# Loads and statistics of the next image's first strips moved to an earlier stage, column means moved beside the sampling, group products cut from nine blocks to seven

## The chip, the cores and the metric

The kernel runs on one core of a Trainium2 chip. The metric is the device time of one execution in microseconds (us); smaller is better. TensorE (PE) has a granted clock of 1.2 or 2.4 GHz; the profile gives it as a share of full speed.

## The reference

The input `x` is (4, 384, 56, 56), float32. Two residual layers follow each other. Cut to what matters:

```python
def _gn(v, G=32, eps=1e-5):            # group norm: 32 groups of 12 channels, over the image
    g = v.reshape(B_, G, C_ // G, H_, W_)
    m = mean(g, axis=(2, 3, 4)); s = var(g, axis=(2, 3, 4))
    return ((g - m) / sqrt(s + eps)).reshape(v.shape)

x = x + layer0(_gn(x))   # depthwise 3x3 convs give value, query (56x56), key, offsets (28x28);
                         # value is sampled bilinearly at tanh(offsets), then attention without
                         # softmax (query x key, x sampled value) and a 384x384 output weight
x = x + layer1(_gn(x))   # layernorm + fc1 (384->1536), silu, fc2; qkv, normalised q and k,
                         # k^T v state per head, normalised output, projection
```

Layer 0 thus needs the mean and variance of every 12-channel group of the raw input before its convolutions; layer 1 needs the same of layer 0's output. fc1's weight is scaled by the layernorm's gain and has its column means taken off, once per launch.

## The kernel before

Channels lie on partitions in three chunks of 128 (`KC = 3`). An image is cut into seven strips of 8 rows, `T = 448` pixels (`STRIPS = 7`). Every engine's program is written out by hand, and the engines meet at semaphores; the order of the calls in each engine's block is the order of its work.

**Stages.** Image 0's layer 0 is a stage of its own (the lead-in, in the text below also "the front"). In it TensorE does nineteen strips of depthwise convolution with diagonal weights (`front_taps`, L826) while VectorE does the rest of the convolutions as units of eight taps each (`unit_conv`, L2086; units 0 to 3 are values, 4 to 6 queries; units 0 to 5 are half images, unit 6 two strips). Each value unit is transposed by TensorE, copied by ScalarE in four pieces into `VP` (L1486), and stored by SyncE's queue into `pair_scr` (`store_front_values`, L409). ScalarE's fourth piece reuses the first piece's buffer, so it waits for the first piece's store to land; only then does it start the unit two further on (`front_unit_start`, L1477). When the last store has landed, GpSimd issues fourteen indirect loads of sample points (`gather`, L666), two for each of seven tiles. VectorE mixes each tile (`sample_tile`, L1989 and L1992), TensorE multiplies it with the keys (`key_value`, L898); after the seventh come `key_value_heads` (MT, L1998), `key_value_out` (L942), and `W2TL`.

**The strip loop of layer 0.** Then seven strips follow (`project_strip` on TensorE). For strip t: SyncE loads queries `CQ` (L430) and the residual `CX` (L433); ScalarE rounds `CH` (`project_high`, L1559); VectorE makes `CL` (`project_low`, L2011); TensorE does 27 matmuls of 448 columns (L780 to L782); VectorE adds into `CX` (`project_add`, L2018) and takes statistics of the sum (L2021); SyncE stores `CX` into `x_scr` (L471). In SyncE's program `CQ` of strip t+2 is loaded in the turn of strip t, behind the store of strip t-1, which waits for that strip's additions. TensorE's strip t+1 uses the banks of strip t, and so waits for its additions. In the same loop VectorE also does `centre_columns` (L2094) in three strips, TensorE `column_means` (L808) after the first three strips, and both are followed by ScalarE's `W1H` (L1596).

**The statistics of the next image's input.** ScalarE's queue loads seven strips of `x` of image 1 into three rotating buffers `X0S` (`load_x0`, L329), and VectorE takes their statistics (`strip_stats`, L1901) inside the strip loop. For later images the same is done elsewhere with `X0Q`.

**The group norm's coefficients.** `gn_coefs` on VectorE and `gn_groups` on TensorE (L766, L774) work in turn: two sets of nine small matmul blocks (3 output chunks x 3 input chunks, a 128x128 block of the group matrix each, 4 columns) and short VectorE steps between them. This happens five times in a launch: at its start, behind the strip loop of image 0, and at the end of the second layer of images 0, 1 and 2 (the tails), among fc1 and fc2 matmuls. After it, `kv_start` normalises the first tile of layer 1 and TensorE starts its key and value products (L985 to L987).

Of the kernel before, what the change touches and what calls it, by code (L numbers as in the profile page):

```python
# [12 lines left out]
P = 128  # L13
C, H, W = 384, 56, 56
KC = C // P
# [58 lines left out]
def build(nc, d, out):  # L74
# [22 lines left out]
    with ctx:  # L97
# [159 lines left out]
        at = [base2]  # L257
        X0S = sb("X0S", [P, 3, KC, T], at=at)
        assert at[0] <= stats_at
# [64 lines left out]

        def load_x0(eng, g, t):

            if t >= 3:
                eng.wait_ge(s["x0bn"], g * STRIPS + t - 2)
            eng.dma_start(X0S[:, t % 3, :, :].rearrange("p k (r w) -> p k r w", w=W),  # L329
                          xin_v[g, :, :, 1 + t * RS:1 + (t + 1) * RS, :]).then_inc(s[f"x0_ld{t % 3}"], 16)  # L330
# [39 lines left out]
        def _(sp):  # L370
# [108 lines left out]
            for u in range(2, 4):  # L479
                store_front_values(u)  # L480
            for u in (4, 5):
                sp.wait_ge(s[("q_st", "q_st1")[u % 2]], (FQ - STRIPS) // 2 * 16)
                store_front_queries(u)
# [5 lines left out]
            load_queries(0)  # L489
            load_queries(1)  # L490
# [255 lines left out]
        def _(pe):  # L746
# [13 lines left out]
            def gn_groups(g, pa, pb, between=None):  # L760

                pe.wait_ge(s["grp_ld"], g * 16 + 16)
                pe.wait_ge(s["gn_st"], g + 1)
                for ko in range(KC):
                    for ki in range(KC):
                        last = mm(pa[:, 4 * ko:4 * ko + 4], grp[:, ki, ko * P:(ko + 1) * P],  # L766
                                  gst[:, ki, :, :].rearrange("p s c -> p (s c)"), start=(ki == 0), stop=(ki == KC - 1))
                last.then_inc(s["gn_mm"], 1)
                if between is not None:
                    between()  # L770
                pe.wait_ge(s["gn_dev"], g + 1)
                for ko in range(KC):
                    for ki in range(KC):
                        last = mm(pb[:, 4 * ko:4 * ko + 4], grp[:, ki, ko * P:(ko + 1) * P],  # L774
                                  gdev[:, ki, :, :].rearrange("p s c -> p (s c)"), start=(ki == 0), stop=(ki == KC - 1))
                last.then_inc(s["gn_mm2"], 1)
# [182 lines left out]
            for t in range(len(SUM_AT), STRIPS):  # L959
                key_value(0, t, VSP)  # L960
            key_value_out(0)
            for t in range(STRIPS):
                project_strip(0, t)
                if t < KC:
                    column_means(t)
# [405 lines left out]
        def _(act):  # L1371
# [217 lines left out]
            load_x0(act, 1, 0)  # L1589
            load_x0(act, 1, 1)  # L1590
            for t in range(2, STRIPS):
                load_x0(act, 1, t)
                project_high(0, t)
                if t == STRIPS - 2:
                    act.wait_ge(s["set_ctr"], 1)
                    fn(W1H[:, :, :], fc1w[:, :, :], ACT.Copy).then_inc(s["w_h"], 1)  # L1596
# [288 lines left out]
        def _(dve):  # L1885
# [10 lines left out]
            def strip_stats(g, t, x=None):  # L1896

                x = X0S[:, t % 3, :, :] if x is None else x
# [232 lines left out]
            unit_conv(4, 3, 6)  # L2131
            for t in range(4):
                sample_tile(0, t, GP, VSP)
            unit_conv(5, 1, 8)
            unit_conv(6, 1, 8)
# [12 lines left out]
            for t in range(STRIPS):  # L2148
                if t == STRIPS - 1:
                    strip_stats(1, t)  # L2150
                project_add(0, t)
                if t + 2 < STRIPS:
                    project_low(0, t + 2)
                if 1 <= t <= KC:
                    centre_columns(t - 1)
                if t < STRIPS - 1:
                    strip_stats(1, t)
# [433 lines left out]
```

## Time and profile before

| what | value |
|---|---|
| median of 3 runs | 2768.92 us (2767.82 to 2769.37) |
| profiled execution, its own time | 2791.05 us |
| its span | 2789.2 us |
| PE busy | 2687.2 us, 96% |
| DVE (VectorE) busy | 1978.9 us, 71% |
| ACT (ScalarE) busy | 1169.6 us, 42% |
| mean granted TensorE clock | 0.969 |

The profiled execution is 22.1 us longer than the median of the runs, so differences are worked out inside it and then laid to the median. The page's 40 slices show TensorE full nearly everywhere except in the first 320 us, where DMA traffic is at its highest.

### The profile page before, as it was taken

The page shows a single profiled execution, that of the slowest core. Times are in us where ns is not written, and L with a number is a line of the kernel's source. Part 1 is how long each engine was busy: PE and PEld are TensorE (multiplying, and loading weights), DVE is VectorE, ACT ScalarE, POOL GpSimd, SP SyncE. Part 2 cuts the span into 40 slices and gives each one's busy share as a digit, 9 for nine tenths or more (in the row PEclk, how much of TensorE's full clock was granted, in tenths as well). Part 3 has the DMA queues.
Part 4 walks back from the last instruction along what each step waited for, and adds up shares of the span by engine and source line. Part 5 has one row for each costly group of instructions (what it writes and reads, how often), then busy time and mean ns, then how long its engine had stood idle before and what let it go on. Part 6 is the DMA issues. An engine that isn't in the chain of part 4 may idle for free.

```text
span 2789.2 us, 36724 instructions
## 1 busy us (share of the span) xinstructions
PE 2687.2 (96%) x14382; PEld 2444.5 (88%) x14382; DVE 1978.9 (71%) x2513; ACT 1169.6 (42%) x2035; POOL 655.7 (24%) x219
## 2 busy tenths in 40 slices
PE   6998799999999999999999999999999999999999
PEld 4556799999998899999998899999998899999998
DVE  4988785988887685988887685988887534434343
ACT  3432465444442465444442366444442253333332
POOL 0020142222232043222223042322224033211210
PEclk8998899999999999999999999999999999999999
DMA  5257643343338642334337743333346632112110
GB/s 224 59 151 246 207 129 83 105 114 114 102 108 258 215 132 75 103 106 115 123 91 231 241 140 84 102 102 102 104 124 204 232 101 70 44 44 57 44 43 30
DMA packets 208249, 345.52 MB, mean 124 GB/s; under 512 B 24272, under 2 KB 191824, under 8 KB 205392
## 3 DMA queue, kind: packets, MB, share of 16 engines
q1 hardware_dynamic: 182048, 309.87, 34.3%
q10 hardware_dynamic: 21552, 14.05, 3.7%
q0 software_dynamic: 4480, 19.27, 2.4%
q8 instruction: 115, 1.88, 0.3%
q14 instruction: 54, 0.44, 0.1%
HBM read 239.59 MB, written 103.56 MB: 123 GB/s over the span
## 4 chain that ended last, share of the span: by engine, by line
PE 74%; DMA 7%; issue 7%; DVE 5%; POOL 4%; ACT 2%; SPq 0%; ACTq 0%; DVEq 0%; POOLq 0%
PE bank L780 16%; PE bank L781 16%; PE bank L782 16%; PE bank L826 3%; PE bank L985 3%; PE bank L987 3%; PE bank L986 3%; PE bank L1008 3%; PE bank L1176 3%; DMA r_scr<-rr 3%; POOL rq L702 2%; PE bank L1162 2%; DVE AC L2391 1%; PE bank L1120 1%; POOL ro L706 1%
## 5 line engine op out<-in xcount | busy, mean ns | idle before, releaser
L1750 ACT ACTIVATE S<-bank,b1p 128x448 f32<-128x448 f32 x336 | 212.4, 632 | 819.5 <-PE bank L782 752.5
L2391 DVE SCALAR_TENSOR_TENSOR AC<-XV,wfold,AC 128x1568 f32<-128x1568 f32 x288 | 530.0, 1846 | 11.5 <-ACT AC L1782 8.9
L780 PE MATMUL bank<-SH,W2H 128*128 128x448 f32 x1008 | 389.9, 387 | 0.2
L780 PE MATMUL bank<-XRH,W1H 128*128 128x448 f32 x1008 | 376.8, 374 | 1.3 <-ACT S L1750 1.3
L781 PE MATMUL bank<-SL,W2H 128*128 128x448 f32 x1008 | 374.0, 371 | 0.0
L782 PE MATMUL bank<-SH,W2L 128*128 128x448 f32 x1008 | 373.7, 371 | 0.0
L781 PE MATMUL bank<-XRL,W1H 128*128 128x448 f32 x1008 | 373.2, 370 | 0.0
L782 PE MATMUL bank<-XRH,W1L 128*128 128x448 f32 x1008 | 371.9, 369 | 0.0
L702 POOL TENSOR_TENSOR rq<-qn,nhalf 112x32 f32<-112x32 f32 x28 | 181.9, 6498 | 481.0 <-DVE qn L2330 481.0
L2360 DVE TENSOR_TENSOR SL<-S,SH 128x448 fp32r<-128x448 f32 x336 | 207.1, 618 | 87.7 <-ACT SH L1753 87.7
L706 POOL TENSOR_TENSOR ro<-on,nhalf 112x32 f32<-112x32 f32 x28 | 180.2, 6434 | 298.7 <-DVE on L2351 298.6
L694 POOL TENSOR_TENSOR rk<-kn,nhalf 128x16 f32<-128x16 f32 (+1 forms) x64 | 169.8, 2667 | 272.0 <-DVE kn L2173 272.0
L985 PE MATMUL bank<-WKVH,XH 128*128 128x384 f32 (+1 forms) x600 | 209.5, 349 | 14.9 <-DVE XL L2030 13.5
L780 PEld LDWEIGHTS bank<-XRH,W1H 128*128 128x128 f32 x1008 | 193.5, 192 | 18.5 <-ACT S L1750 2.1
L1753 ACT ACTIVATE SH<-S 128x448 fp32r<-128x448 f32 x336 | 194.4, 578 | 31.7 <-ACT S L1750 1.1
L782 PEld LDWEIGHTS bank<-XRH,W1L 128*128 128x128 f32 x1008 | 192.1, 191 | 17.4
L782 PEld LDWEIGHTS bank<-SH,W2L 128*128 128x128 f32 x1008 | 194.6, 193 | 14.4
L780 PEld LDWEIGHTS bank<-SH,W2H 128*128 128x128 f32 x1008 | 193.8, 192 | 14.6 <-DVE SL L2360 1.3
L781 PEld LDWEIGHTS bank<-XRL,W1H 128*128 128x128 f32 x1008 | 192.7, 191 | 15.2
L781 PEld LDWEIGHTS bank<-SL,W2H 128*128 128x128 f32 x1008 | 194.7, 193 | 12.2 <-issue 0.6
L986 PE MATMUL bank<-WKVL,XH 128*128 128x384 f32 (+1 forms) x600 | 203.9, 340 | 0.0
L987 PE MATMUL bank<-WKVH,XL 128*128 128x384 f32 (+1 forms) x600 | 203.9, 340 | 0.0
(227 smaller groups left out, 5169.0 us busy)
## 6 DMA issues: line engine op xcount, KB each, us to landing
XV<-in_xp SPq DMA_DIRECT2D x36, 870.0 KB, 6.9
XC<-in_xp SPq DMA_DIRECT2D x13, 1682.0 KB, 9.2
CQ<-q_scr SPq DMA_DIRECT2D x28, 672.0 KB
CX<-in_x SPq DMA_DIRECT2D x28, 672.0 KB, 5.2
x_scr<-CX SPq DMA_DIRECT2D x28, 672.0 KB, 5.7
X<-x_scr SPq DMA_DIRECT2D x28, 672.0 KB, 4.2
V<-v_scr SPq DMA_DIRECT2D x28, 672.0 KB, 7.3
Y<-x_scr SPq DMA_DIRECT2D x28, 672.0 KB
```

What stands on the lines that cost most here:

```text
L702: pool.tensor_tensor(rq[:, :], qn[:, :], nhalf[0:TS, :], ALU.pow).then_inc(s["rq_s"], 1)
L706: pool.tensor_tensor(ro[:, :], on[:, :], nhalf[0:TS, :], ALU.pow).then_inc(s["ro_s"], 1)
L780: mm(o, wh, xh, start=first, stop=False)
L781: mm(o, wh, xl, start=False, stop=False)
L782: return mm(o, wl, xh, start=False, stop=stop)
L985: mm(p, xh, WKVH[:, k, c0:c0 + C], start=(k == 0), stop=False)
L986: mm(p, xh, WKVL[:, k, c0:c0 + C], start=False, stop=False)
L987: last = mm(p, xl, WKVH[:, k, c0:c0 + C], start=False, stop=(k == KC - 1))
L1750: fn(S[:, j % 2, :], bank[j % 2][:, 0:T], ACT.Silu, bias=b1p[:, j:j + 1]).then_inc(s["s_s"], 1)
L1753: fn(SH[:, j % 3, :], S[:, j % 2, :], ACT.Copy).then_inc(s["sh"], 1)
L2360: tt(SL[:, j % 3, :], S[:, j % 2, :], f(SH[:, j % 3, :]), ALU.subtract).then_inc(s["sl"], 1)
L2391: stt(o, XV[h][:, ky:ky + HR, kx:kx + W], wfold[:, kind, k, 3 * ky + kx:3 * ky + kx + 1], o, ALU.mult, ALU.add).then_inc(s["va"], 1)
```

## The change

1. `X0S` and `load_x0` go. The seven strips of image 1 are loaded by SyncE's queue into the single buffer `CQ1`, which the queries use only later; each load but the first waits for the statistics of the strip before it. The loads stand ahead of or between the stores of value units 2 and 3, and the last five ahead of the stores of query units 4 and 5.
2. VectorE's seven `strip_stats(1, t, CQ1)` move from the strip loop to between the convolution units 4, 5 and 6; the first two taps of unit 5 move ahead of the first four sample tiles.
3. `column_means` 0 to 2 move from behind the first three strips to ahead of the last three `key_value`; `centre_columns` goes one strip earlier, ahead of the additions.
4. `load_queries(1)` waits for the last strip's statistics too.
5. In every `gn_groups`, each output chunk multiplies only neighbouring input chunks: seven blocks in place of nine. The two left out (0 with 2) are zero in the group matrix, as a group has 12 neighbouring channels.

```diff
-        def load_x0(eng, g, t):
-            if t >= 3:
-                eng.wait_ge(s["x0bn"], g * STRIPS + t - 2)
-            eng.dma_start(X0S[:, t % 3, :, :]..., xin_v[g, :, :, 1 + t * RS:1 + (t + 1) * RS, :])...
...
+            def load_first_strip(t):
+                if t >= 1:
+                    sp.wait_ge(s["x0bn"], STRIPS + t)
+                sp.dma_start(CQ1[:, :, :].rearrange("p k (r w) -> p k r w", w=W),
+                             xin_v[1, :, :, 1 + t * RS:1 + (t + 1) * RS, :]).then_inc(s[f"x0_ld{t % 3}"], 16)
+            sp.wait_ge(s["wkv_st"], 32)
+            load_first_strip(0)
+            store_front_values(2)
+            load_first_strip(1)
+            store_front_values(3)
+            for t in range(2, STRIPS):
+                load_first_strip(t)
+            sp.wait_ge(s["q_st"], (FQ - STRIPS) // 2 * 16)
+            store_front_queries(4)
+            sp.wait_ge(s["q_st1"], (FQ - STRIPS) // 2 * 16)
+            store_front_queries(5)
...
             load_queries(0)
+            sp.wait_ge(s["x0bn"], 2 * STRIPS)
             load_queries(1)
...
+                near = ((0, 1), (0, 1, 2), (1, 2))
                 for ko in range(KC):
-                    for ki in range(KC):
+                    for ki in near[ko]:
...
             for t in range(len(SUM_AT), STRIPS):
+                column_means(t - len(SUM_AT))
                 key_value(0, t, VSP)
             for t in range(STRIPS):
                 project_strip(0, t)
-                if t < KC:
-                    column_means(t)
...
             sampling_points(0)
-            unit_conv(4, 3, 6)
+            strip_stats(1, 0, CQ1)
+            unit_conv(4, 3, 3)
+            strip_stats(1, 1, CQ1)
+            unit_conv(4, 6, 3)
+            strip_stats(1, 2, CQ1)
+            unit_conv(5, 1, 2)
             for t in range(4):
                 sample_tile(0, t, GP, VSP)
-            unit_conv(5, 1, 8)
-            unit_conv(6, 1, 8)
+            strip_stats(1, 3, CQ1)
+            unit_conv(5, 3, 3)
+            strip_stats(1, 4, CQ1)
+            unit_conv(5, 6, 3)
+            strip_stats(1, 5, CQ1)
+            unit_conv(6, 1, 4)
+            strip_stats(1, 6, CQ1)
+            unit_conv(6, 5, 4)
...
             for t in range(STRIPS):
-                if t == STRIPS - 1:
-                    strip_stats(1, t)
+                if t < KC:
+                    centre_columns(t)
                 project_add(0, t)
                 if t + 2 < STRIPS:
                     project_low(0, t + 2)
-                if 1 <= t <= KC:
-                    centre_columns(t - 1)
-                if t < STRIPS - 1:
-                    strip_stats(1, t)
```

## Rows read from the trace of the kernel before

**Rows 1.** Stages: us, busy us per engine (x instructions), PE clock, DMA share, GB/s.

```profile
160.00:165.00 5.00, 5.00 (x17) 2.65 (x16) 4.89 (x4) 4.29 (x5) 0.00 (x0) 1.00 1.00 271
...
200.00:205.00 5.00, 5.00 (x21) 2.94 (x21) 3.15 (x6) 0.00 (x0) 3.78 (x5) 1.00 1.02 291
...
242.00:304.00 62.00, 53.65 (x213) 42.67 (x213) 52.89 (x85) 12.62 (x10) 0.00 (x0) 0.92 0.94 320
280.00:285.00 5.00, 5.00 (x14) 4.44 (x14) 4.06 (x7) 1.32 (x1) 0.00 (x0) 0.50 0.96 264
...
321.00:960.00 639.00, 629.77 (x3493) 590.67 (x3494) 508.02 (x627) 290.25 (x510) 169.50 (x53) 0.98 0.45 135
```

**Rows 2.** VectorE's strip loop: start, us, operation, [idle before, releaser].

```profile
275.61 1.88 DVE L2094 TENSOR_TENSOR fc1w<-fc1w,bank 128x512 f32<-128x512 f32 x3
277.41 1.67 DVE L1901 BATCH_NORM_STATS2 bst<-X0S 128x6 f32<-128x448 f32 x3
279.00 1.66 DVE L2018 TENSOR_TENSOR CX<-CX,bank 128x448 f32<-128x448 f32 x3
...
283.19 1.56 DVE L2011 TENSOR_TENSOR CL<-CQ,CH 128x1344 fp32r<-128x1344 f32 x1 [0.94 <-ACT CH L1559]
...
304.82 1.36 DVE L1908 BATCH_NORM_AGGREGATE gst<-bst 128x2 f32<-128x42 f32 x6
```

**Rows 3.** Transfer sizes from 140 to 320 us, and SyncE's and ScalarE's timeline.

```profile
X0S<-in_x ACTq DMA_DIRECT2D x7, 672.0 KB, 10.2
...
160.25 23.74 SPq L409 DMA_DIRECT2D pair_scr<-VP  x8
...
264.20 0.51 SPq L430 DMA_DIRECT2D CQ<-q_scr  x1
...
272.78 1.33 ACT L1559 ACTIVATE CH<-CQ 128x1344 fp32r<-128x1344 f32 x1 [7.62 <-DMA CQ<-q_scr]
```

**Rows 4.** ScalarE in the front: the pieces of the value units, and the scaling of fc1's weight.

```profile
167.90 0.60 ACT L1486 ACTIVATE VP<-bank 112x512 f32<-112x512 f32 x1 [3.60 <-DMA pair_scr<-VP]
168.40 1.96 ACT L1477 ACTIVATE AP<-XC,bfold,wfold 128x784 f32<-128x784 f32 x2
...
228.38 4.51 ACT L1584 ACTIVATE fc1w<-fc1w,lng 128x1536 f32<-128x1536 f32 x3 [7.09 <-PE bank L797]
```

**Rows 5.** The chain that ended last, around the gathers: start, us, what.

```profile
183.69 2.47 DMA pair_scr<-VP
...
187.24 2.72 POOL GP L666
```

**Rows 6.** VectorE in the front.

```profile
170.44 3.73 DVE L2086 SCALAR_TENSOR_TENSOR AP<-XC,wfold,AP 128x1568 f32<-128x1568 f32 x2
...
196.18 0.42 DVE L1989 TENSOR_SCALAR VSP<-GP,W 112x384 f32<-112x384 f32 x1 [7.21 <-DMA GP<-pair_scr,IX]
...
205.96 0.42 DVE L1989 TENSOR_SCALAR VSP<-GP,W 112x384 f32<-112x384 f32 x1 [2.65 <-PE bank L898]
...
224.42 8.28 DVE L2086 SCALAR_TENSOR_TENSOR AP<-XC,wfold,AP 128x896 f32<-128x896 f32 x7
...
241.31 0.56 DVE L1998 TENSOR_TENSOR MT<-bank,head_s 128x384 f32<-128x384 f32 x1 [1.74 <-PE bank L898]
```

**Rows 7.** TensorE's timeline, before and in the strip loop.

```profile
235.04 1.65 PE L898 MATMUL bank<-KT,VSP 112*128 112x128 f32 x6 [6.70 <-DVE VSP L1992]
...
246.79 0.47 PE L780 MATMUL bank<-CH,W2TH 128*128 128x448 f32 x1 [1.17 <-DVE W2TL L2005]
...
268.42 2.74 PE L808 MATMUL bank<-fc1w,ones 128*128 128x512 f32 x6
...
279.74 0.71 PE L780 MATMUL bank<-CH,W2TH 128*128 128x448 f32 x1 [3.02 <-DVE CX L2018]
```

**Rows 8.** TensorE's group products: behind the strip loop, and in the first tail.

```profile
306.33 3.97 PE L766 MATMUL bank<-gst,grp_s 128*128 128x4 f32 x18 [4.62 <-DVE gst L1908]
...
935.80 2.06 PE L766 MATMUL bank<-gst,grp_s 128*128 128x4 f32 x18
```

More of the change, by code:

```diff
@@ L256, in build @@
         OTP, GEP = sb("OTP", [TK, STRIPS, C], at=[shared]), sb("GEP", [P, KC, NK], at=[base2 + 10368])
-        at = [base2]
-        X0S = sb("X0S", [P, 3, KC, T], at=at)
-        assert at[0] <= stats_at
         GP = [sb(f"GP{i}", [TK, 2, 2, C], at=[a]) for i, a in enumerate((base2, base2 + 6144, xc0_at, xc0_at + 6144))]
@@ L323, in x0_at @@
             return 16 + slot_at(g - 1, t, 3, 16)
-        def load_x0(eng, g, t):
-            if t >= 3:
-                eng.wait_ge(s["x0bn"], g * STRIPS + t - 2)
-            eng.dma_start(X0S[:, t % 3, :, :].rearrange("p k (r w) -> p k r w", w=W),
-                          xin_v[g, :, :, 1 + t * RS:1 + (t + 1) * RS, :]).then_inc(s[f"x0_ld{t % 3}"], 16)
         KEYS_AT = (3, 5, 7)
@@ L478, in _ @@
             load_output_weight()
[L479 to L483, printed above, removed]
+            def load_first_strip(t):
[14 more added lines that the diff above has]
+            store_front_queries(5)
             sp.wait_ge(s["va"], HEAD + 7 * 8)
@@ L764, in gn_groups @@
                 for ko in range(KC):
-                    for ki in range(KC):
+                    for ki in near[ko]:
                         last = mm(pa[:, 4 * ko:4 * ko + 4], grp[:, ki, ko * P:(ko + 1) * P],
-                                  gst[:, ki, :, :].rearrange("p s c -> p (s c)"), start=(ki == 0), stop=(ki == KC - 1))
+                                  gst[:, ki, :, :].rearrange("p s c -> p (s c)"), start=(ki == near[ko][0]), stop=(ki == near[ko][-1]))
                 last.then_inc(s["gn_mm"], 1)
@@ L772, in gn_groups @@
                 for ko in range(KC):
-                    for ki in range(KC):
+                    for ki in near[ko]:
                         last = mm(pb[:, 4 * ko:4 * ko + 4], grp[:, ki, ko * P:(ko + 1) * P],
-                                  gdev[:, ki, :, :].rearrange("p s c -> p (s c)"), start=(ki == 0), stop=(ki == KC - 1))
+                                  gdev[:, ki, :, :].rearrange("p s c -> p (s c)"), start=(ki == near[ko][0]), stop=(ki == near[ko][-1]))
                 last.then_inc(s["gn_mm2"], 1)
@@ L1588, in _ @@
             key_value_high(0)
-            load_x0(act, 1, 0)
-            load_x0(act, 1, 1)
             for t in range(2, STRIPS):
-                load_x0(act, 1, t)
                 project_high(0, t)
@@ L1894, in _, with strip_stats @@
             dve.tensor_reduce(wsum[:, :, :], wconv[:, :, :, :], AX.X, ALU.add)
-            def strip_stats(g, t, x=None):
-                x = X0S[:, t % 3, :, :] if x is None else x
+            def strip_stats(g, t, x):
                 dve.wait_ge(s[f"x0_ld{t % 3}"], x0_at(g, t))
```

## The prediction

> **What bounds the kernel now.** I read the stages first. From 321 us on TensorE is busy 98 to 99% of the time [rows 1], so that only work taken off TensorE itself shortens that part. The lead-in is different: from 242 to 304 us, the strip loop, the DMA engines are busy 94% and move 320 GB/s, VectorE is busy 85%, TensorE 87% [rows 1]. Every microsecond taken off the lead-in's chain is a microsecond off the launch, since TensorE's full stretch simply starts earlier.
>
> The timeline of VectorE shows the loop's turn: columns centred (1.8 us from start to start), next image's statistics 1.6, additions 1.6, own statistics the same 1.6, low part 1.5: 8.1 us, with a wait of 0.94 for ScalarE's CH before the low part [rows 2]. ScalarE in turn waits for the query load: one is issued at 264.20 and used at 272.78, 8.6 us later, and ScalarE had stood 7.62 us [rows 3]. So two things bind side by side, VectorE's turn and the latency of a load in a full DMA system. TensorE's 27 matmuls, about 0.2 us apart at full clock, are 5.4 us. The loop takes from 246.79, strip 0's first matmul [rows 7], to 304.82, the aggregation [rows 2]: 58.0 us.
>
> **What leaves the loop.** Seven strips' statistics (7 x 1.6 = 11.1 us of VectorE), seven loads of 672 KB, which is 688,128 bytes each (4.8 MB, or 15 us at 320 GB/s) [rows 1, 3], and three column means (2.2 us each of TensorE) [rows 7]. Centring stays, one strip earlier.
>
> I work the loop out anew from the first strip's additions, x1a(0) = 0, which come 6.3 us after its first matmul. The query load of strip t+2 is issued 0.4 us after the additions of strip t-1 and lands L later; then CH 1.4, low part 1.5, centring 1.8 (strips 1 and 2), additions 1.6, own statistics 1.6 [rows 2, 3]. For L: two transfers at 320 GB/s are 4.3 us, and a small store takes 2.5 to land [rows 5], so 6.8 is the low end; 8.6, as now, or 9.5 with ill luck, the high one. I take 8.0, nearer to today's row, since a strip still moves three transfers (2.06 MB, 6.5 us). With 8.0 the additions of strips 1 to 6 end at 6.5, 14.7, 19.4, 27.5, 32.9 and 36.1 (strip 6's high part also waits behind ScalarE's W1H, 4.1 us), the last statistics at 37.7. 6.3 + 37.7 = 44.0 against 58.0: **-14.0 us**. With 6.8 it is 41.6 (-16.4), with 9.5 it is 47 (-11). The volume agrees: up to the last query load 16 transfers, the group matrix and part of WKVL, 12.4 MB, take 39 us from the first residual load, and that load lies some 6 us ahead of the loop.
>
> **What this costs in the front.** The moved loads are queued on SyncE, ahead of stores that others wait for.
>
> Load 0 stands right ahead of unit 2's stores, issued from 160.25 on [rows 3]. There the engines are full at 271 GB/s [rows 1], so it holds those stores back by 688,128 / 271 = 2.5 us. ScalarE's piece at 167.90 waits for exactly such a landing (3.60 us), and behind it in ScalarE's order is the start of unit 4 at 168.40 [rows 4]. VectorE began that unit's taps at 170.44, as it was ready [rows 6]: now about 172.9.
>
> Then 3.7 us of two taps, 2.3 of sampling points, 1.6 of statistics: the first strip's statistics end at about 180.6, and only then does SyncE issue load 1 and, behind it, unit 3's stores. Their first piece lands at 181.1 + 2.4 + 2.5 = 186.0, the fourth copy follows at 186.0 to 186.6, its store lands 2.5 later at 189.1 against 186.2 [rows 5]: the gathers start **3 us** late.
>
> Load 3 is issued when the third statistics end (180.6 + 2 x (3 x 1.88 + 1.6) = 195.0) and falls among the gathers, when the engines are full at 291 GB/s [rows 1]: 2.4 us more for the fourth tile, which now starts at 205.96 [rows 6] + 3 + 2.4 = 211.3. Two statistics, the second and third, and two taps of unit 5 fit into VectorE's idle 7.21 us before the first tile [rows 6]; VectorE is ready at 198.7, the tile at 199.2.
>
> After the fourth tile VectorE has four statistics (6.3 us) more and two taps (3.7) fewer than now: the fifth tile goes from 232.7 [rows 6] to 232.7 + 5.4 + 2.6 = 240.7. TensorE's front also ends 5.4 later, fc1's weight is then scaled in 4.5 us [rows 4] from 233.8 to 238.3, and column means 0 runs until the fifth tile is there. The other two (2.2 each) alternate with the last key products; the last product ends at about 249.8 where it ended at 241.3 [rows 6]: **+8.5 us** for the start of the loop. Without any DMA delay only VectorE's 2.6 and 0.5 of TensorE's remain, +3.1; with the column means at half clock, 4.3 each, it is +12.5. The row at 235.04 is such a half-clock stretch (1.65 us for six small matmuls, after 6.70 idle [rows 7]).
>
> The moves of the query stores: they were issued at about 223 us; now they wait for the sixth statistics, at about 229.5. Nobody asks for them before unit 6's own store, at about 240.5 now, so they cost nothing; without unit 6 behind them it would be those 6 us.
>
> **Group products.** Seven blocks of nine; 18 records become 14. Behind the loop a set takes 3.97 us [rows 8], so 0.88 less, twice: **-1.8**. VectorE's fc1 low part, 1.7 us, lies inside both and remains covered. At the launch's start only the first set is uncovered (the second ends before VectorE's WKVL), at 1.9 us: -0.4. In the three tails a set takes 1.9 us on a TensorE that never stops [rows 1, 8]: 0.42 x 2 x 3 = -2.5. Together **-4.7**. The bounds here are narrow, -3 to -5, the lower if the tails' saving is lost to waits for VectorE.
>
> **Sum.** -14.0 + 8.5 - 4.7 = -10.2 us. Against the profiled execution's own 2791.05 that is 2780.8; its distance to the median of the runs, 22.1 us, is not touched: 2768.9 - 10.2 = **2758.7 us**. Ends: 3.1 - 16.4 - 4.7 = -18 (2751), and 12.5 - 11 - 3 = -1.5 (2767.4).
>
> **Rivals.**
> (A) The clock falls in the loop. At 279.74 TensorE had stood 3.02 us [rows 7] and then began 14 matmuls in 5 us at a granted clock of 0.50, the lower of its two levels, 1.2 GHz [rows 1]: 0.37 us each where 0.2 is usual, for over half of a strip, 2.6 us lost. In my loop the gaps reach 2.7 us (strips 4 to 5), because the column means no longer fill them, and between the output weight's products and strip 0 there are about 3. One or two falls, +2.6 to +5: 2761 to 2764. Chance 0.22.
> (B) It falls in every strip. Then a strip takes 27 x 0.37 = 10.0 us, the loop 6.3 + 4 + 6 x 10.6 = 74 in place of 44, and the launch is slower: 8.5 + 16 - 4.7 = +20, 2789; with it in half of the strips 2774. It decides from gaps of some 3 us in each strip, that is an L above 9. This is also the rule of the skill's page "TensorE: Matmul & The Clock Gate", section "HAM oscillation": a loop that waits for DMA between short bursts starts each burst cold. Against it: over the whole loop the granted clock is 0.92, with one such fall [rows 1]. Chance 0.07.
> (C) The loads hurt nobody in the front, since the stores slip through: +3.1, gathers still at 187. Against it is the 3.60 us wait. 2751 to 2754. Chance 0.15.
> (D) The loop's latency stays, because the transfers bunch anyway (L = 9.5 to 10) and the front's delay is 10 or more: -1 to -4, 2765 to 2768. Chance 0.13.
>
> **How the numbers follow.** The forecast's own range, 2754 to 2763, has 0.43. Within 0.2% (5.5 us, about what a measurement can tell from no change) lie part of A, and D. Faster: 0.43 + 0.15 + 0.14 of A = 0.72; same: 0.08 + 0.13 = 0.21; slower: 0.07. The range takes in C and D: 2749 to 2769.
>
> **What would show it.** Unit 4's taps near 173, the first gather near 190, MT near 250, strip loop 44 us long with no X0S in it, DMA share below 0.94, sets of 14 records at L766. I am wrong if the gathers start at 187, if the loop's turn stays at 8 us, or if the clock shows 0.5 within the loop.

## The result, and the profile after

The changed kernel takes 2769.71 us (median of 20 runs, 2763.07 to 2777.19). The kernel before takes 2777.73 us over 20 runs. Three of these are the runs that the prediction had (2768.92); the other 17 have a median of 2779.91. The ratio of the two kernels is 0.9976, with a 95% interval from 0.9965 to 0.9987. That is 6.7 us less (3.6 to 9.7). The forecast was 10.2 us less. The sign holds and the size was too large. The absolute time lies 11.0 us above the forecast of 2758.7, and 8.8 of these come from the level of the kernel before, which the prediction took from three runs.

The profiled execution of the changed kernel has a span of 2775.3 us against 2789.2. The 13.9 us between them are more than the ratio gives, and the section on the experiments shows why a single pair of spans says little. The lead-in can be read more sharply. I measure it from one fixed event, VectorE's copy of the sampling offsets (`OFF`, at 170.14 us before and 168.69 after). Up to there the two kernels differ only in the first two group sets and in load 0's issue at 158.53; over all profiled executions the copy came between 168.7 and 170.8 us. "Layer 1" below is the first write of its normalised tile `XL`.

| stretch, us | before | after | difference | forecast |
|---|---|---|---|---|
| offsets' copy to strip 0's first matmul | 76.65 | 85.99 | +9.3 | +8.5 |
| strip loop, first matmul to aggregation | 58.03 | 45.36 | -12.7 | -14.0 |
| aggregation to layer 1 (two group sets) | 15.08 | 13.37 | -1.7 | -1.8 |
| together | 149.8 | 144.7 | -5.0 | -7.3 |

With 2.7 us for the three tails and 0.4 for the start (below) this makes -8.1, inside the measured interval. The interval just misses -10.2.

The loop as a stage of the changed kernel, with busy time of PE, PEld, DVE, ACT and POOL, PE clock, DMA share and GB/s; to be read against the third row of [rows 1]:

```profile
242.00:304.00 62.00, 51.40 (x238) 43.28 (x236) 48.90 (x78) 14.62 (x11) 0.00 (x0) 0.97 0.86 290
```

The DMA share fell from 0.94 to 0.86 and the granted clock rose from 0.92 to 0.97. In this execution rivals A and B, in which the clock falls in the loop, did not come: TensorE had stood 2.06 us before strip 0 and 0.78 to 1.42 between strips, and the granted clock was 1.00 throughout the loop. In other executions of the same loop code it fell at strip 0, as the run `nine_blocks` below shows.

VectorE, from the front into the loop (start, mean duration, line, operation, [idle before it, what ended it]), against [rows 2 and 6]:

```profile
171.02 3.74 DVE L2087 SCALAR_TENSOR_TENSOR AP<-XC,wfold,AP 128x1568 f32<-128x1568 f32 x2 [1.95 <-ACT AP L1482]
...
202.47 0.54 DVE L1990 TENSOR_SCALAR VSP<-GP,W 112x384 f32<-112x384 f32 x1 [3.03 <-DMA GP<-pair_scr,IX]
...
207.94 0.42 DVE L1990 TENSOR_SCALAR VSP<-GP,W 112x384 f32<-112x384 f32 x1
...
237.82 0.42 DVE L1990 TENSOR_SCALAR VSP<-GP,W 112x384 f32<-112x384 f32 x1
...
249.74 0.56 DVE L1999 TENSOR_TENSOR MT<-bank,head_s 128x384 f32<-128x384 f32 x1 [4.01 <-PE bank L904]
...
297.74 0.62 DVE L2019 TENSOR_TENSOR CX<-CX,bank 128x448 f32<-128x448 f32 x1 [1.18 <-PE bank L788]
...
300.04 1.36 DVE L1909 BATCH_NORM_AGGREGATE gst<-bst 128x2 f32<-128x42 f32 x6
```

The signs named in the prediction are there: unit 4's taps at 171.02 (2.0 us later, counted from the offsets' copy), MT at 249.74, no `X0S` in the loop. But MT stood 4.01 us for TensorE, where it had stood 1.74 [rows 6]. That is the first surprise, and TensorE's and ScalarE's rows explain it:

```profile
232.08 4.51 ACT L1589 ACTIVATE fc1w<-fc1w,lng 128x1536 f32<-128x1536 f32 x3 [6.58 <-PE bank L803]
```

```profile
236.64 5.49 PE L814 MATMUL bank<-fc1w,ones 128*128 128x512 f32 x6 [4.60 <-ACT fc1w L1589]
...
248.87 0.83 PE L904 MATMUL bank<-KT,VSP 112*128 112x128 f32 x6
...
254.68 0.47 PE L786 MATMUL bank<-CH,W2TH 128*128 128x448 f32 x1 [2.06 <-DVE W2TL L2006]
...
292.06 0.44 PE L786 MATMUL bank<-CH,W2TH 128*128 128x448 f32 x1 [0.96 <-DVE CX L2019]
...
301.55 3.12 PE L772 MATMUL bank<-gst,grp_s 128*128 128x4 f32 x14 [3.84 <-DVE gst L1909]
...
929.66 1.62 PE L772 MATMUL bank<-gst,grp_s 128*128 128x4 f32 x14
```

The column means wait 4.60 us for the scaling of fc1's weight, and after that idle time the first six take 5.49 us, 0.92 each, at a granted clock of 0.50, where six took 2.74 in the loop [rows 7]. The group sets have 14 records and take 3.12 us where they took 3.97, and 1.62 where they took 2.06 [rows 8].

SyncE and ScalarE in the front and in the loop, against [rows 3, 4]; first the issues, then the pieces and `CH`:

```profile
178.66 0.40 SPq L474 DMA_DIRECT2D CQ<-in_x  x1
...
179.63 6.55 SPq L399 DMA_DIRECT2D pair_scr<-VP  x4
...
273.91 0.36 SPq L461 DMA_DIRECT2D x_scr<-CX  x1
...
274.32 0.49 SPq L420 DMA_DIRECT2D CQ<-q_scr  x1
...
280.19 0.37 SPq L423 DMA_DIRECT2D CX<-in_x  x1
...
281.14 0.49 SPq L420 DMA_DIRECT2D CQ<-q_scr  x1
```

```profile
168.53 0.60 ACT L1491 ACTIVATE VP<-bank 112x512 f32<-112x512 f32 x1 [5.96 <-DMA pair_scr<-VP]
...
185.26 0.60 ACT L1491 ACTIVATE VP<-bank 112x512 f32<-112x512 f32 x1 [2.70 <-DMA pair_scr<-VP]
...
281.85 1.33 ACT L1564 ACTIVATE CH<-CQ 128x1344 fp32r<-128x1344 f32 x1 [6.17 <-DMA CQ<-q_scr]
```

Load 0 ahead of unit 2's stores made the wait of the fourth piece 5.96 where it was 3.60 [rows 4]: +2.4, as worked out. Load 1 is issued at 178.66, 1 us ahead of unit 3's stores. `CH` still waits 6.17 us for its query load, issued at 274.32 and used at 281.85: 7.5 us.

### The profile page after: what moved, and what is told of

Read it like the earlier page. It is cut to its first block, busy times and chain, and to the rows that moved or that the text cites. A ratio compares the mean times of both kernels' runs of the same rounds, so it can differ in the third digit from the quotient of the medians.

```text
span 2775.3 us, 36644 instructions
## 1 busy us (share of the span) xinstructions
PE 2678.9 (97%) x14342; PEld 2434.4 (88%) x14342; DVE 1979.2 (71%) x2513; ACT 1167.8 (42%) x2035; POOL 660.1 (24%) x219
## 4 chain that ended last, share of the span: by engine, by line
PE 74%; DMA 8%; issue 7%; DVE 4%; POOL 3%; ACT 3%; SPq 0%; ACTq 0%; DVEq 0%; POOLq 0%
PE bank L786 16%; PE bank L787 16%; PE bank L788 16%; PE bank L832 4%; PE bank L990 3%; PE bank L992 3%; PE bank L991 3%; PE bank L1181 3%; PE bank L1013 3%; DMA r_scr<-rr 2%; PE bank L1167 2%; POOL rq L707 1%; DMA X0Q<-in_x 1%; DMA X<-x_scr 1%; PE bank L1125 1%
## 5 line engine op out<-in xcount | busy, mean ns | idle before, releaser
L990 PE MATMUL bank<-WKVH,XH 128*128 128x384 f32 (+1 forms) x600 | 207.1, 345 | 13.6 <-DVE XL L2031 12.2
```

The costliest lines, as they stand in the source:

```text
L990: mm(p, xh, WKVH[:, k, c0:c0 + C], start=(k == 0), stop=False)
```

## The experiments

Each ratio is against the kernel before, run in turns with it on the same chip. Because the ratios' intervals are some 9 us wide, I compare the lead-in's stretches as well, always from the offsets' copy. Where the code is the same, the front repeats to about 2 us (83.8 to 86.0 in four runs) and the loop to about 3 (44.1 to 47.0 in five). A smaller difference between two executions shows nothing by itself.

### Which part of the change gives what

**groups_only**: the kernel before with the seven-block group products alone.

```diff
-                    for ki in range(KC):
+                    for ki in near[ko]:
```

> The kernel before with only the group products cut from nine blocks to seven. Theory 1 (each saved record is time on the chain, in the tails too): the two sets behind the strip loop take 3.1 us each in place of 4.0, the tails' six sets 1.5 in place of 1.9; -1.8 behind the loop, -2.5 in the tails, -0.4 at the start, together -4.7 us. Rival: in the tails the records saved are given back in the next wait for VectorE, so only -2.2 us. The strip loop from its first matmul to the aggregation stays at 58 us in both.

Measured: ratio 0.9967 [0.9950, 0.9983], -9.2 us (-4.7 to -13.9). The sets behind the loop take 3.12 and 3.15 us (3.97 and 4.00 before), the aggregation to layer 1 13.4 (15.1). In the tails a set takes 1.62 (2.06), 0.45 less from start to start, six times: 2.7 us. Loop 57.1, front 75.9. The sets account for 4.8 us with the 0.4 at the start, the forecast's term; the rest of the 9.2 lies in no set and is within what the ratio can err.

**nine_blocks**: the changed kernel with all nine blocks, so the moves alone.

```diff
-                    for ki in near[ko]:
+                    for ki in range(KC):
```

> The changed kernel with nine blocks again. Theory 1: what the moved loads, statistics and column means give by themselves, front +8 to +9.5 and loop -12.7, that is -3 to -5 us against the kernel before. Rival (the moves are neutral and all of the gain is the group products): within 1 us of the kernel before. Loop 45 us, MT at about 251 in both.

Measured: 0.9981 [0.9962, 1.0000], -5.3 us (0 to -10.6). Loop 44.6, front 83.8, aggregation to layer 1 15.1. From the offsets' copy to layer 1 it is 143.5, 6.2 less than before; the changed kernel's own stretch, with its 1.7 us of group products taken out, is 3.3 less than before. With the group products in both, the changed kernel's stretch is only 1.6 less than that of `groups_only` (144.7 against 146.3). So the lead-in shows 2 to 6 us for the moves, with up to 3 of uncertainty. The whole times don't settle it: this interval reaches 0, and the changed kernel's ratio (0.9976) is no better than that of `groups_only` (0.9967).

Strip 0 of the loop shows what rival A had in mind. These are its first 5.5 us in the changed kernel and in this run, with PE clock, DMA share and GB/s at the end, and this run's first matmul:

```profile
254.68:260.18 5.50, 5.50 (x27) 5.17 (x28) 5.48 (x9) 0.00 (x0) 0.00 (x0) 1.00 1.00 391
```

```profile
254.45:259.95 5.50, 5.50 (x19) 4.99 (x20) 4.95 (x8) 0.00 (x0) 0.00 (x0) 0.69 1.00 394
...
254.45 0.53 PE L785 MATMUL bank<-CH,W2TH 128*128 128x448 f32 x1 [2.06 <-DVE W2TL L2005]
```

TensorE had stood 0.74 and 2.06 us just before in both. Strip 0's additions end 6.3 us after its first matmul at a clock of 1.00, and 7.9 at 0.69: 1.6 us lost. `load0_early`, `idle_loads` and `idle_behind` show the same 0.69 there, `act_queue` and `load3_late` 1.00. What decides between the two is not shown.

**means_back**: column means and centring back in the loop, loads and statistics stay out.

```diff
             for t in range(len(SUM_AT), STRIPS):
-                column_means(t - len(SUM_AT))
                 key_value(0, t, VSP)
...
                 project_strip(0, t)
+                if t < KC:
+                    column_means(t)
```

> The changed kernel with the column means behind the first three strips and the centring one strip later, as before. Theory 1: column means ahead of the last key products hold up MT, because they wait for fc1's scaling and the first runs at half clock; without them the last key product ends some 4 us earlier (MT at 245.5 in place of 249.7), and the loop takes 3 to 4 us more (48 to 50 us), since TensorE then needs 7.6 us in each of three strips; sum 0 to -1 us against the changed kernel. Rival (the means fill time in which TensorE waits anyway, as the moved place suggests): MT stays, loop +4, the kernel 4 us slower than the changed one.

Measured: 0.9988 [0.9973, 1.0003]. The loop takes 52.9 us, 7.6 more than the changed kernel's, while the front is only 1.6 shorter. Of the 7.6, 1.9 are strip 0 at a granted clock of 0.62; the other 5.7 are the means. From the offsets' copy to layer 1 it is 149.8, as long as before the change and 3.5 longer than in `groups_only` (146.3). So the loads and statistics, moved without the means, gain nothing. I had expected the means to cost the loop 4 us at most. TensorE's strips with a mean take 8.1 us where they took 6.4, and it has no gap in them; `CH` then waits for TensorE and not for its load:

```profile
278.18 1.32 ACT L1565 ACTIVATE CH<-CQ 128x1344 fp32r<-128x1344 f32 x1 [6.66 <-PE bank L788]
```

```profile
248.30 0.56 DVE L2000 TENSOR_TENSOR MT<-bank,head_s 128x384 f32<-128x384 f32 x1 [1.74 <-PE bank L904]
```

MT waits 1.74 again and comes 2.75 us sooner after the offsets' copy than in the changed kernel (78.3 against 81.05), but only 0.6 sooner than in `nine_blocks` (78.9), whose front is the changed kernel's. What the means cost the front is thus between 0.6 and 2.75 us.

**means_only**: the kernel before with the means and the centring moved, and the scaling early as in `bias_early` below, with the group products too; loads and statistics stay in the loop.

> The kernel before with the group products, the column means and centring moved, and bias sums early, but with the loads and statistics of image 1 still in the strip loop. Theory 1 (the moves of loads and statistics earn 12.7 us in the loop for 5 to 9 in the front): MT at 240 to 241, loop 54 to 58 us, from the offsets' copy to the first low part 145 to 147 us against 140.1 in bias_early; 3 to 6 us slower than bias_early. Rival (the moves of the statistics are worth nothing once the column means leave the loop): loop 50 us or less, 140 us or less from copy to low part.

Measured: 0.9998 [0.9986, 1.0010]; MT at 241.4, loop 56.3, offsets' copy to layer 1 149.0. Against `groups_only` the loop is only 0.8 us shorter and the front 3.5 longer, so the means moved alone, too, gain nothing. TensorE had stood 3.80 us before strip 0 and did the strip at a granted clock of 0.50, which cost 2.6 us; without that the loop would be 3.4 shorter.

```profile
248.03 0.74 PE L781 MATMUL bank<-CH,W2TH 128*128 128x448 f32 x1 [3.80 <-DVE W2TL L2014]
```

So taking the means out is worth 5.7 us when the loads and statistics are out of the loop, and 3.4 when they are in, both without the loss of clock. The parts do not add. With the statistics in, VectorE's turn and the loads bind as well, and part of TensorE's means lies beside them; with them out, TensorE's own chain binds.

Against `bias_early` below, which differs from this run only in the loads and statistics, the loop is 11.5 us longer, 2.6 of them from the clock, and the front 3.0 shorter. With the means out of the way, moving the loads and statistics is thus worth 8.9 us from copy to layer 1 (149.0 against 140.05).

**idle_loads** and **idle_behind**: the changed kernel with seven loads of the old size put back into the loop on ScalarE's queue, into an unused buffer, with no statistics. In the first a load is issued ahead of each `CH` from strip 2 on, and so is its wait for the buffer's last load; in the second both stand behind it. Two loads stand ahead of the loop in both.

```diff
             for t in range(2, STRIPS):
+                if t >= 3:
+                    act.wait_ge(s[(...)[t % 3]], ...)     # the buffer's load before has landed
+                idle_load(t)
                 project_high(0, t)
```

> The changed kernel with the seven loads issued in the strip loop again, on ScalarE's queue, into a buffer that nobody reads; the statistics stay in the front. It leaves out nothing and adds 4.8 MB. Theory 1 (latency of the query loads in full DMA engines sets the loop, beside VectorE): the wait of CH for CQ grows, loop 48 to 52 us in place of 45.4. Rival (VectorE's turn alone made the loop 58 us, transfers are hidden): the loop stays at 45 to 46 us.

Measured (one run, 2777.22 us): loop 53.4. But at two strips `CH` waited for the idle load itself, an artefact of the order:

```profile
272.13 1.33 ACT L1565 ACTIVATE CH<-CQ 128x1344 fp32r<-128x1344 f32 x1 [6.21 <-DMA X0S<-in_x]
```

> The changed kernel with seven idle loads in the strip loop as in the run idle_loads, but each is issued behind that strip's high part instead of ahead of it, so that the wait for a free buffer does not stand ahead of a high part that is ready. Theory 1 (bytes in the DMA engines lengthen the query loads): ScalarE waits for CQ, not for the idle buffer, and the loop is 50 to 54 us, as with idle_loads (53.4). Rival (the 8 us of idle_loads were the buffer wait on ScalarE, an artefact): the loop is 46 to 48 us.

Measured (one run, 2782.09 us): loop 49.8, 4.4 more than without the loads. From strip 2 on `CH` waits for the queries alone:

```profile
277.35 1.33 ACT L1565 ACTIVATE CH<-CQ 128x1344 fp32r<-128x1344 f32 x1 [6.89 <-DMA CQ<-q_scr]
...
304.15 1.36 DVE L1925 BATCH_NORM_AGGREGATE gst<-bst 128x2 f32<-128x42 f32 x6
```

So 4.4 of the 12.7 us come back with no instruction of VectorE added, just under the 50 to 54 expected. But strip 0 ran at a clock of 0.69 here (1.6 us). Against the runs with that same fall and without the loads, 44.6 in `nine_blocks` and 47.0 in `load0_early`, it is 2.7 to 5.2. This is one run, and about 3 to 5 us is what it shows for the transfers.

### What the front pays, and for what

**load0_early**: load 0 issued 96 us earlier (at 62.27 us in place of 158.53), ahead of the first front strip's store.

```diff
+            load_first_strip(0)
             store_front_strip(0)
...
-            sp.wait_ge(s["wkv_st"], 32)
-            load_first_strip(0)
             store_front_values(2)
```

> The changed kernel with load 0 issued right after the weights' store, some 100 us earlier, so that it stands ahead of no store that is waited for. Theory 1 (the queue position of load 0 and, through the statistics, of load 1 holds up the value stores and so the gathers): unit 4's taps start with no wait for ScalarE, 2 us earlier; the first gather is issued at 187 to 188 in place of 189.5; MT comes 2 us earlier; -2 us against the changed kernel. Rival (TensorE's bias sums, scaling and column means set MT, not the tiles): the gathers move but MT stays within 0.5 us, and so does the time.

Measured: 0.9957 [0.9941, 0.9974]; unit 4's taps at 171.8, 1.0 after the offsets' copy (2.3 in the changed kernel, 0.3 before); first gather at 191.0, 20.2 after it (20.8 and 17.1); MT at 250.3, 79.5 after the copy (81.05 in the changed kernel). Unit 4 wins 1.3 us, the gathers 0.6 and MT 1.5, which is no more than the same front varies by, and the copy to layer 1 takes 144.9 us against 144.7. So the gain expected at the gathers did not come. The rows show why:

```profile
180.12 0.40 SPq L411 DMA_DIRECT2D CQ<-in_x  x1
...
180.56 7.21 SPq L399 DMA_DIRECT2D pair_scr<-VP  x4
```

```profile
169.32 0.60 ACT L1490 ACTIVATE VP<-bank 112x512 f32<-112x512 f32 x1 [4.29 <-DMA pair_scr<-VP]
...
186.84 0.60 ACT L1490 ACTIVATE VP<-bank 112x512 f32<-112x512 f32 x1 [3.50 <-DMA pair_scr<-VP]
```

It is load 1, right ahead of unit 3's stores (0.44 us), that holds the gathers back: unit 3's piece still waits 3.50.

**act_queue**: loads 0 and 1 issued by ScalarE's queue, behind three pieces of units 2 and 3.

```diff
-            load_first_strip(0)
             store_front_values(2)
-            load_first_strip(1)
             store_front_values(3)
...
+                if i in UNIT_AT[2:]:
+                    first_strip(UNIT_AT.index(i) - 2)
```

> The changed kernel with loads 0 and 1 issued from ScalarE's queue at about the instants at which SyncE's queue issued them. Theory 1 (in one queue the stores go behind the load's whole length, between two queues the engines take turns): the fourth piece of unit 2 waits 4 to 5 us in place of 5.96, that of unit 3 0.5 to 2 in place of 2.70, first gather at 187.5 to 188.5 in place of 189.5. Rival (only the bytes in the engines count, whatever the queue): 5.5 to 6 and 2.5 to 3 us, first gather at 189 to 190.

Measured (one run, 2770.47 us), ScalarE:

```profile
170.06 0.60 ACT L1488 ACTIVATE VP<-bank 112x512 f32<-112x512 f32 x1 [5.55 <-DMA pair_scr<-VP]
...
183.81 0.60 ACT L1488 ACTIVATE VP<-bank 112x512 f32<-112x512 f32 x1 [0.98 <-DMA pair_scr<-VP]
```

Unit 3's piece waits 0.98 where it waited 2.70, and the first gather starts 18.4 us after the offsets' copy (20.8 in the changed kernel, 17.1 before). Unit 2's piece waits 5.55, hardly less than 5.96. So what the prediction drew from the rule that queues take turns is borne out for one load and not for the other. MT comes 77.4 after the copy, against 81.05: TensorE's front ends earlier, so the scaling does too, and the means start 65.1 after the copy where they started 67.9. From the copy to layer 1 it is 139.4 us, 5.3 less than in the changed kernel and the shortest of all; as one run it shows no more than a hint.

**load3_late**: load 3 held back until the fourth tile is sampled.

```diff
             for t in range(2, STRIPS):
+                if t == 3:
+                    sp.wait_ge(s["vs_s"], 4)
                 load_first_strip(t)
```

> The changed kernel with load 3 issued only after the fourth tile is mixed. Theory 1 (load 3 takes the gathers' share of the DMA engines): second tile's wait 1 us or less in place of 3.0, fourth tile 1 to 2.4 us earlier relative to the first gather; MT the same or earlier by under 1 us, since the means hold it. Rival (load 3 is not among the gathers' rivals): the tiles come as in the changed kernel, 13.0 us from first gather's issue to second tile.

Measured (one run, 2776.62 us), VectorE:

```profile
202.07 0.42 DVE L1992 TENSOR_SCALAR VSP<-GP,W 112x384 f32<-112x384 f32 x1 [0.80 <-DMA GP<-pair_scr,IX]
...
218.50 1.68 DVE L1904 BATCH_NORM_STATS2 bst<-CQ 128x6 f32<-128x448 f32 x3 [8.03 <-DMA CQ<-in_x]
```

The second tile waits 0.80 where it waited 3.03, and starts 10.6 us after the first gather instead of 13.0: the load does cost the gathers 2.4 us, the forecast's term. The other runs agree in the direction: 9.7 to 11.3 us where no load falls among the gathers, 11.8 to 14.9 where load 3 does. But VectorE then stands 8.03 for that load, and MT comes 6 us later.

**bias_early**: the second half of fc1's bias sums and the scaling move forward, the scaling to ScalarE's place 48 of the front; all three column means stand ahead of the fifth tile's key products, and those of the first four tiles come three places earlier.

```diff
+                if i == BIAS_AT:                 # 42, was behind the front
+                    bias_sums(JC // 2, JC)
...
-                column_means(t - len(SUM_AT))
+                if t == len(SUM_AT):
+                    for q in range(KC):
+                        column_means(q)
...
+                elif i == 48:
+                    scale_fc1()
```

> The changed kernel with the second half of the bias sums moved ahead, behind unit 3's transposes, fc1's scaling behind them, and all three column means right behind the last front strip; key products of the first four tiles three places earlier, so that they keep their time. Theory 1 (in the changed kernel the means, which wait for bias sums and scaling, hold up the last key products): the last product ends right behind the last tile, MT 1.7 us after the sample tile's end in place of 4.0, at 245 to 246.5, 3 to 4 us earlier, time -3.5 us against the changed kernel. Rival (VectorE's own load in the front sets MT): MT within 1 us of the changed kernel.

Measured: 0.9951 [0.9935, 0.9967], -13.6 us (-9.2 to -18.1); median 2762.76 (8 runs). It is faster than the kernel before and, by the two ratios, faster than the changed kernel by 6.9 us, give or take some 5. From `groups_only` the ratios do not tell it apart.

```profile
229.83 7.96 PE L814 MATMUL bank<-fc1w,ones 128*128 128x512 f32 x18 [0.82 <-ACT QA L1431]
...
239.21 0.94 PE L904 MATMUL bank<-KT,VSP 112*128 112x128 f32 x6 [1.41 <-DVE VSP L2002]
...
243.79 1.65 PE L904 MATMUL bank<-KT,VSP 112*128 112x128 f32 x6 [1.36 <-DVE VSP L2002]
```

```profile
245.48 0.56 DVE L2008 TENSOR_TENSOR MT<-bank,head_s 128x384 f32<-128x384 f32 x1 [1.74 <-PE bank L904]
...
296.33 1.36 DVE L1918 BATCH_NORM_AGGREGATE gst<-bst 128x2 f32<-128x42 f32 x6
```

The means run in one piece, 0.44 us a matmul, while TensorE has nothing else; MT waits 1.74 again and comes 4.8 us earlier after the copy than in the changed kernel (76.2 against 81.05), 2.7 earlier than in `nine_blocks`. The offsets' copy to layer 1 is 140.05, against 144.7 in the changed kernel, 146.3 in `groups_only` and 149.8 before.

**early_stats**: `bias_early`, and load 0 early, each statistics placed so that load 1 is issued well ahead of unit 3's stores, and load 3 late.

```diff
             sampling_offsets(0)
+            strip_stats(1, 0, CQ1)
             unit_conv(4, 1, 2)
             sampling_points(0)
-            strip_stats(1, 0, CQ1)
-            unit_conv(4, 3, 3)
             strip_stats(1, 1, CQ1)
-            unit_conv(4, 6, 3)
+            unit_conv(4, 3, 6)
```

> As bias_early, and load 0 right behind the weights' store, the first statistics ahead of unit 4's taps (so load 1 is issued at about 172 into idle DMA engines), load 2 behind unit 3's stores, load 3 only after the fourth tile is mixed, the other statistics one place later. Theory 1 (loads queued ahead of stores and among the gathers delay the tiles): first gather at 186.5 to 187.5 in place of 189.5, no wait of the second tile (3.0 us in the changed kernel), the fourth tile at 205 to 206 in place of 208 to 210, MT at 243 to 245; 5 to 7 us faster than the changed kernel. Rival: the gathers are earlier but VectorE, with all seven statistics, still ends at the same time, MT as in bias_early.

Measured: 0.9969 [0.9952, 0.9985]; median 2767.82 (12 runs). The gathers start 17.8 us after the copy, nearly as before the change. MT comes 77.0 after it, where it was 76.2 in `bias_early`.

```profile
206.55 0.42 DVE L2000 TENSOR_SCALAR VSP<-GP,W 112x384 f32<-112x384 f32 x1 [0.54 <-issue]
...
238.80 0.41 DVE L2000 TENSOR_SCALAR VSP<-GP,W 112x384 f32<-112x384 f32 x1
```

The time won at the gathers is gone by the fifth tile: from the fourth tile (206.55) to the fifth (238.80) it is 32.3 us, against 30.1 in `bias_early`. VectorE's work between them is the same, but its statistics wait 3.2 us for loads there (1.47, 0.63 and 1.07) where they waited 1.06.

**bias_act**: `bias_early` with `act_queue`.

> bias_early and act_queue together. Theory 1 (the two delays of the front, means behind fc1's scaling and stores behind loads, are separate): MT at 244 to 245 against 245.5 in bias_early, copy of the offsets to first low part 137 to 139 us against 140.1; 14 to 16 us faster than the kernel before. Rival (once the means are out of the way VectorE's own work sets the last tile, so earlier gathers change nothing): MT and lead-in within 1 us of bias_early, 12 to 14 us faster than before.

Measured: 0.9961 [0.9943, 0.9979]; MT 76.7 after the copy and 141.15 to layer 1, against 76.2 and 140.05. But this is no test of earlier gathers, since they came only 0.5 us earlier (20.1 after the copy, 20.6 in `bias_early`). Unit 3's fourth piece waited a mere 0.57, and then its own store took 5.25 us to land, where it took 2.5 in `bias_early` and 3.2 in `act_queue`: the load on the other queue delayed a store all the same, only a later one. The two landings, from the chain of `bias_act` and of `bias_early`:

```profile
182.82 5.25 DMA pair_scr<-VP
```

```profile
186.26 2.49 DMA pair_scr<-VP
```

### How far a span can be trusted

The second image's stretch is the same code in `load0_early` and `means_back`, whose difference lies wholly in the lead-in. The two windows, from each one's first tail to its second:

```profile
935.00:1564.00 629.00, 615.38 (x3447) 576.40 (x3448) 502.22 (x620) 285.87 (x500) 169.48 (x53) 0.99 0.45 137
```

```profile
938.60:1579.50 640.90, 623.51 (x3449) 583.67 (x3448) 502.47 (x620) 285.94 (x500) 168.07 (x53) 0.97 0.44 134
```

The same code takes 629.0 us in one and 640.9 in the other, at a granted clock of 0.99 and 0.97, and both ran in turns on one chip. Over all profiled executions the part from layer 1's start to the end varied between 2448 and 2469 us. It was 2469.3 in the profile of before and 2461.9 in that of after; that is the part of the spans' 13.9 us which the change does not explain.

## Where the prediction was right, and which of its steps failed

**The step that failed.** The sum ends in "2768.9 - 10.2", and the 2768.9 is what failed: three runs gave it, where 20 gave 2777.7. That is 8.8 of the 11.0 us by which the changed kernel lies above the forecast, and it puts 2769.7 outside both ranges, 2751 to 2767.4 and 2749 to 2769. A sign of it was on record: the profiled execution of the same kernel stood 22.1 us above the three runs, and the prediction took that distance as fixed, not as spread. Why the level differs stays open. In the terms of the change, +8.5 assumed that MT follows the tiles, where MT waited for matmuls behind the scaling, and the -14.0 left out two steps of the loop; both are below.

**Direction and mechanism.** Right in the main. The lead-in lost 12.7 us in the loop and paid 9.3 in the front, and the group products gave 4.8. The group products' share is seen set by set. That of the moves is shown by the lead-in's stretches (1.6 to 6.2 us) and not by the whole times. `idle_behind` and `means_back` give back parts of the loop's gain.

**Load 0, 2.5 us.** Right: the piece's wait grew by 2.4 and unit 4 began 2.0 later (2.5 forecast). Over all runs that wait is 3.27 to 4.42 us with no load ahead and 5.90 to 6.57 with one on the same queue. The 3.60 us of the rows, which the prediction called in for the queue's rule, stood there without any load ahead and so bore nothing out.

**"The gathers start 3 us late."** Right, 3.7. `load0_early`, `act_queue` and `early_stats` (17.8) show that load 1 causes most of it. The Trainium skill, "DMA: Bandwidth & Descriptors", section "Queues, rings and completion order", says that each DMA engine takes turns between the queues it has work for. The prediction's estimate from it, about half the delay with the load on another queue, is not borne out at unit 2 (5.55 and 6.14 against 5.96). At unit 3 the fourth piece waits less than half (0.98 and 0.57 against 2.70), but the last store then lands in 3.2 and 5.25 us in place of 2.5.

**"Load 3: 2.4 us more for the fourth tile."** The load does cost the gathers 2.4 by one pair of runs (`load3_late`). The fourth tile itself came 3.4 later, not 5.4: it had a wait for TensorE in it before [rows 6], which took up part of the delay.

**The fifth tile, +8.0.** It came 6.7 later: 2.0 less from the fourth tile, 0.6 more between the two (3.2 where 2.6 was forecast), part of it VectorE's waits of 0.52 and 0.25 for loads.

**"+8.5 for the start of the loop."** +9.3, and +7.2 in `nine_blocks`, so the size holds, but for another reason and by luck: the fifth tile came earlier than forecast and MT waited longer. The prediction let the last two means alternate with the key products at full clock and had MT follow the tiles. In fact TensorE stood 4.60 us for the scaled weight, began the means at 0.92 us a matmul, and MT stood 4.01 us for it. I had named the half clock as the upper bound and not taken it. `bias_early` takes that wait away, and MT comes 2.7 to 4.8 sooner. What then sets MT is probably VectorE's work ahead of the last tile: TensorE waits 1.41, 1.36 and 1.36 us for the last three tiles, and `early_stats`, which starts the gathers 2.8 us earlier, does not bring MT forward, though VectorE waits 2.1 us longer for loads there. It was not tried to take one of VectorE's taps or statistics away.

**"With L = 8.0 ... 44.0."** The loop was 45.4. The latency was 5.8 to 7.6 us from issue to use and so better than taken; with 6.8 my recurrence gives 41.6, not 45.4. What failed is the recurrence, which left out two steps worth some 3.6 us, and 44.0 came near because the L taken was too long: two errors that nearly cancel. First, SyncE's order, 1.4 us: the store of strip 2, issued at 273.91, had to land before the residual load went out at 280.19 and the query load behind it at 281.14, 1.8 us after the additions, where I took 0.4. Second, 2.2 us, TensorE's own chain at the end: its last strip's matmuls start at 292.06 and the last addition at 297.74, with waits of 0.86 and 1.18; the loop ends on TensorE's 5.4 us of matmuls, where I took 3.2 between the additions of strips 5 and 6.

**Three parts of the loop's gain.** The prediction listed them side by side. The runs show that they overlap. Without the loss of clock in strip 0 the means are worth 5.7 us in the loop once the rest is out (`means_back`) and 3.4 while it is in (`means_only`); loads and statistics together are worth 8.9 with the means out (`bias_early` against `means_only`), of which the transfers are some 3 to 5 (`idle_behind`). What the statistics alone are worth was not measured.

**Group products, -4.7.** Measured -1.7 behind the loop and 6 x 0.45 = -2.7 in the tails. At the start the second set begins 0.4 sooner after the first. Right.

**Rivals.** A did not come in the profiled execution. It came at strip 0 in four others of the same front and loop, and cost 1.6 us there where the rival had 2.6; with the idle loads in the loop it came a second time (0.62 from 288.0 to 292.5 us in `idle_behind`). It was named for that place, between the output weight's products and strip 0. B came in none. C fails on the first gather (+3.7), D on the latency.

## What to carry to other kernels

Work moved out of a crowded stage is paid for where it lands, and a new neighbour on another engine can set part of the price: here matmuls that had to wait for a scaling nobody had moved with them. When a loop is bound by several chains at once, take one part back at a time; here the loads and statistics without the means, and the means without them, each gained nothing, and together, with the scaling moved too, they shortened the lead-in by 6 us against `groups_only`. Judge small changes by a stretch between two fixed events as well as by whole times, and learn from several executions how far that stretch repeats before reading a difference. A forecast of an absolute time needs a level from more than three runs. Look for loads queued right ahead of stores that somebody waits for; moving them to another engine's queue helped at one place here and not at another.

## What the runs showed of the hardware that was not expected

- The same instructions took between 629.0 and 640.9 us for one image (granted clock 0.99 and 0.97) on the same chip.
- After 4.60 us of idle time TensorE's first six matmuls of 128x512 took 0.92 us each at a granted clock of 0.50, against 0.44 at 1.00 in `bias_early`, where it had stood only 0.82. Over the seven runs with that same wait the six took 4.30 to 5.49 us together.
- In strip 0 of the same loop code, after the same waits of 0.74 and 2.06 us, the granted clock was 1.00 in three executions and 0.69 in four.
- A load of 688,128 bytes on another queue left a store's wait at 5.55 us in one place and cut it from 2.70 to 0.98 in another, where the store behind it then took 3.2 us to land and in a second run 5.25, in place of 2.5.
